# The transposes of the queries behind the whole projection, and the squares ahead of the copy of the queries, in a windowed-attention kernel on one core

## The reference, cut to what matters

```python
# layer 0: x = x + attention(group_norm(x)), in windows of 16 x 16 pixels, 8 heads of 12 channels
qkv = jnp.einsum('oc,bchw->bohw', w_qkv, x)
...
q = _l2norm(q).transpose(0, 1, 3, 2)
k = _l2norm(k)
ksum = k.sum(axis=-1) + EPS
tailor = 1.0 / (ws * ws + jnp.einsum('bhnc,bhc->bhn', q, ksum))
kv = jnp.einsum('bhmn,bhcn->bhmc', k, v)
attn = jnp.einsum('bhnm,bhmc->bhcn', q, kv)
attn = attn + v.sum(axis=-1, keepdims=True)
attn = attn * tailor[:, :, None, :]
...
y = jnp.einsum('oc,bchw->bohw', w_proj, out)
y = (y - mean) * jax.lax.rsqrt(var + BN_EPS)      # over the whole batch
# layer 1: x = x + wavelet_convolution(group_norm(x)), three Haar levels and a 5 x 5 depthwise convolution
```

## Time and profile before

| | |
|---|---|
| time, median of 3 runs | 11901.09 us (11895.07 to 11904.0) |
| time of the profiled execution | 11889.79 us, span 11888.0 us |
| granted TensorE clock, mean | 0.995 |
| TensorE busy | 10743.1 us, 90% |
| VectorE busy | 9364.9 us, 79% |
| ScalarE busy | 6980.0 us, 59% |
| GpSimd busy | 3393.1 us, 29% |

### The profile page before, as it was taken

One profiled execution on the slowest core, in us unless ns is written; L12 is line 12 of the kernel. 1 busy time (PEld: TensorE's weight loads), 2 busy tenths in 40 slices (PEclk: granted clock), 3 DMA queues, 4 the chain that ended last, 5 costly groups with the idle time before them and its releaser, 6 DMA issues. The chain is left out here.

```text
span 11888.0 us, 209663 instructions
## 1 busy us (share of the span) xinstructions
PE 10743.1 (90%) x68680; PEld 9231.7 (78%) x68680; DVE 9364.9 (79%) x16196; ACT 6980.0 (59%) x11653; POOL 3393.1 (29%) x2756
## 2 busy tenths in 40 slices
PE   0006999999999999999969999999999999999999
PEld 0005888888888888888858888888888888888888
DVE  6667888888888888888867777777777777777777
ACT  0005888888888888888844444555554444444554
POOL 1002444444444444444421222222222222222221
PEclk9999999999999999999979999999999999999999
DMA  9993222222222222222236666666666666666665
GB/s 233 217 219 88 80 80 78 82 75 85 75 85 75 85 75 79 81 76 84 75 76 147 147 147 149 149 148 148 149 149 149 147 147 147 147 147 147 149 149 125
DMA packets 1149490, 1452.08 MB, mean 122 GB/s; under 512 B 202079, under 2 KB 1111711, under 8 KB 1111967
## 3 DMA queue, kind: packets, MB, share of 16 engines
q1 hardware_dynamic: 1147743, 1442.74, 50.3%
q10 hardware_dynamic: 1376, 6.13, 0.1%
HBM read 1040.06 MB, written 408.56 MB: 122 GB/s over the span
## 5 line engine op out<-in xcount | busy, mean ns | idle before, releaser
L1076 PE MATMUL ps_w<-zb,mat 128*128 128x512 f32 x4800 | 1925.5, 401 | 0.1
L1078 PE MATMUL ps_w<-zb,mat 128*128 128x512 f32 x4800 | 1907.8, 397 | 0.0
L1077 PE MATMUL ps_w<-zb,mat 128*128 128x512 f32 x4800 | 1907.2, 397 | 0.0
L1029 ACT ACTIVATE z<-x,prm 64x384 f32<-64x384 f32 (+1 forms) x3072 | 1806.3, 659 | 54.7 <-DVE x L1139 47.0
L491 POOL CAST xn_hi<-xs 96x512 fp32r<-96x512 f32 x1024 | 882.6, 862 | 2854.7 <-PE ps_qkv L515 2067.2
L975 POOL CAST mat<-raw 128x1280 fp32r<-128x1280 f32 (+1 forms) x288 | 344.1, 1213 | 4452.5 <-DMA raw<-vec 2641.1
L1201 DVE SCALAR_TENSOR_TENSOR ob<-ps_w,prm,x 64x512 f32<-64x512 f32 x1920 | 1440.3, 750 | 182.6 <-PE ps_w L1119 143.6
L1139 DVE SCALAR_TENSOR_TENSOR x<-yb,prm,xb 128x1024 f32<-128x1024 f32 (+1 forms) x576 | 1120.7, 1997 | 387.0 <-DMA prm<-params 341.2
L513 PE MATMUL ps_qkv<-wqkv_hi,xn_hi 96*128 96x288 f32 x4096 | 1383.7, 338 | 23.3 <-POOL xn_lo L493 20.0
L493 POOL TENSOR_TENSOR xn_lo<-xs,xn_hi 96x512 fp32r<-96x512 f32 x1024 | 1297.8, 1267 | 82.2
L1049 ACT ACTIVATE ll<-ps_ll 128x512 f32<-128x512 f32 x192 | 115.1, 599 | 1882.7 <-PE ps_ll L1084 1882.7
(11 more groups left out here) (138 smaller groups left out, 24172.4 us busy)
## 6 DMA issues: line engine op xcount, KB each, us to landing
xs<-in_x SPq DMA_DIRECT2D x256, 1536.0 KB, 9.1
y_scratch<-ys SPq DMA_DIRECT2D x128, 1536.0 KB, 9.3
out<-ob SPq DMA_DIRECT2D x768, 208.0 KB
xb<-in_x SPq DMA_DIRECT2D x576, 256.0 KB
yb<-y_scratch SPq DMA_DIRECT2D x576, 256.0 KB
raw<-vec SPq DMA_DIRECT2D x192, 320.0 KB, 5.3
raw<-vec SPq DMA_DIRECT2D x384, 160.0 KB, 4.1
xb<-in_x SPq DMA_DIRECT2D x192, 240.0 KB
```

Source lines behind the costliest of these rows:

```text
L1029: last = nc.scalar.activation(z[q * WROWS:(q + 1) * WROWS, ts, b, :], x1[slot(k, g)][rows, pairs, b, q::2], ACT.Identity, scale=prm[k][row ...
L1076: mm(out_, w[HI], xx[HI], start=start, stop=False)
L1077: mm(out_, w[HI], xx[LO], start=False, stop=False)
L1078: return mm(out_, w[LO], xx[HI], start=False, stop=stop)
```

## The change

`project` no longer leaves its fourth group behind `turn_q`: TensorE issues all twelve matmuls of the projection, signals `qkv_ready`, and then issues the four transposes of the queries. On ScalarE `squares(u)` stands ahead of `copy_q(u-1)`. Nothing is added or removed, no wait and no buffer is changed.

```diff
@@ ScalarE, step @@
+                    if inside_(at, 0):
+                        squares(u, at == 0)
                     if inside_(at, 1):
                         copy_q(u - 1, (j - 1) % 2, at is not None and at - 1 < 2)
                     if inside_(at, 0):
-                        squares(u, at == 0)
                         copy_tok(u, j % 2, at is not None and at < 2)
@@ TensorE @@
-                def project(u, slot, gs):
+                def project(u, slot):
 
-                    for g in gs:
+                    for g in range(TG):
@@ TensorE, step @@
-                        project(u, j % 2, range(0, TG - 1))
+                        project(u, j % 2).then_inc(qkv_ready, 1)
                     if inside_(at, 1):
                         turn_q(u - 1, (j - 1) % 2, at is not None and at - 1 < 2)
-                    if inside_(at, 0):
-                        project(u, j % 2, range(TG - 1, TG)).then_inc(qkv_ready, 1)
```

## The result

The change makes the kernel slower: 11937.29 us (median of 7 runs, 11934.86 to 11944.88) against 11900.35 us (median of 7 runs, 11895.07 to 11904.0) for the kernel before. The ratio is 1.0033, 95% interval 1.0021 to 1.0045. The profiled execution took 11934.86 us against 11889.79, 45 us more. The difference is small, 0.3%, but clear of the runs' scatter: the slowest of the runs before is 31 us faster than the fastest after. In the rows of the experiments the numbers are again shifted by up to three, by each experiment's own edit; tiles and operations are the same.

The account below looks back on a forecast made before the run. TensorE's own work was taken to bound stage 2. Place 1 (22), place 3 (22), place 0 (22), turns (23) and ScalarE (-5) gave +84 us on 11889.8, 11974; predicted median 11985, 8-in-10 range 11910 to 12070.

Parts of the forecast that it names:

- the rival in which VectorE keeps places 0 and 3: Places 0 and 3: VectorE keeps its turn at both or one of them, 11941 or 11963 us; chance 0.22.
- GpSimd is first by 0.05 at place 1 and by a hair at places 0 and 3: Port race there: GpSimd's earlier cast starts before VectorE's line 621 or 642, so all three places are lost.
- the 0.45 us by which `qkv_ready` comes earlier: End of the projection, every place: last matmul starts at 2861.65 instead of 2862.10, without the transposes ahead of it.
- TensorE's order: Stage 2 steps: query transposes with `numerators` right behind take 0.44 us for four; new order costs nothing within 0.02 us.
- ScalarE: Squares ahead of `copy_q`: what follows starts 0.05 us earlier, GpSimd's late split of place 7 too, about 5 us gained.
- The price at place 1: Line 621 waits for GpSimd's cast, so line 551 starts 0.17 us later; 128 x 0.17 = 22 us.
- The turns: Loop's turns: line 621 waits for GpSimd's subtraction, line 558 comes later; a mean turn loses 0.77 us, 30 lose 23.
- Rival D: Not slower: at turns the fourth group's matmuls fill TensorE's wait, 30 x 0.39 = 12 us, giving 11884; chance 0.08.
- rival E: Places 2, 4 and 5: GpSimd wins the port there too, adding 78 us, 12063; chance 0.12.
- The price at place 0: Line 642 waits for GpSimd's cast, so line 558's transpose comes later; 0.22 us a step, 98 x 0.22 = 22 us.
- The lock's rule: Port pair shared by VectorE and GpSimd: whichever starts first holds it for the whole instruction, so places 0, 1, 3 are lost.

Follow-up runs that it names:

- e3: The full change with GpSimd's split also waiting for the transposes of the queries, against the kernel before: 11886.15 us against 11894.77, ratio 0.9994.
- e10: The full change with three tiny VectorE sums between line 621 and line 642, against the kernel before: 12036.1 us against 11896.13, ratio 1.0118.
- e5: The full change with three tiny VectorE sums behind the reciprocal of line 617, against the kernel before: 11940.67 us against 11899.15, ratio 1.0035.
- e7: The full change with GpSimd's split waiting for the query transposes and, at a strip's first unit, the unit keys; against the kernel before: 11868.56 us against 11899.15.
- e6: The kernel before with the split of a strip's first unit also waiting for the unit keys: 11878.76 us against 11899.15, ratio 0.9982.

## Why the prediction was wrong

The direction and the cause were right: the loss is GpSimd's earlier cast and subtraction, which take the port from VectorE. The size was not, and of the places one (place 0) was wrong and one (place 3) mostly so. I gave 11985 us (+84) with 11941 to 11963 for the rival in which VectorE keeps places 0 and 3; measured is 11937 (+37), or 45 us more between the profiled executions, for which the sum was made. That is close to the rival, which had 0.22.

The step that failed is "GpSimd is first by 0.05 at place 1 and by a hair at places 0 and 3". It rests on the 0.45 us by which `qkv_ready` comes earlier, read from one step. Over all steps the last projection matmul starts 1.98 us into the step before and 1.55 after, 0.43 us earlier. The cast starts 2.44 us into it before and 2.01 after (medians), 0.43 earlier; at place 0 it is 2.437 and 2.032, 0.41. Those two to four hundredths turn a race by a hair around. Counted in the trace after, VectorE lost at place 0 in 0 of 96 steps (I had all: 22 us; it is 2), at place 3 in 35 of 128 (22 us; it is 8), and at place 1 in 53 of 96 without those behind a turn, in 30 of 31 behind one (22 us together; it is 18). What splits place 1 is TensorE: the last projection matmul starts 1.53 or 1.54 us into the step in all 53 steps with VectorE held, and 1.56 or 1.57 us into it in 39 of the 43 others, as the two steps shown do (3042.37 and 2963.14). Some 44 us of the sum, places 0 and 3, hung on ties of 0.01 us, read from one step each, and were counted in full; 8 of them came, at place 3.

Point by point otherwise. TensorE's order: four transposes with `numerators` behind take 0.44 us, as taken. ScalarE: `copy_tok` starts 0.02 to 0.04 us earlier instead of 0.05, and place 7 gained 0.033 x 128 = 4 us instead of 5. The price at place 1: 0.17 forecast, 0.18 in the steps shown. With 53 of 96 steps and not all, place 1 comes to 18 us near the 22 forecast partly since the steps with VectorE let in lose 0.03 us too. The turns: 0.77 forecast, 0.75 measured, 23 us both, but in part by luck: the forecast path, line 620 behind the subtraction, is that of 23 turns in 29, and the other six lose nearly the same by line 641. Rival D made it hang on line 620 not being held at the turns; where it was not, the turn was lost all the same. Its gain of 0.39 us a turn is not to be had either, as e3 shows. Places 2, 4 and 5 stayed with VectorE, so rival E falls there; but what it describes, GpSimd getting in between the product of keys and line 641, is what happened at those six turns. The price at place 0 could not be seen in the change; in e10 it was 0.19 for 0.22.

The lock's rule in the Trainium skill (SBUF — State Buffer, "SBUF: two separate sides"), that whoever starts first gets the port pair, held in the trace after. There are 89 steps in which the cast's start lies 0.01 to 0.04 us ahead of line 620's, and 29 behind a turn with 0.23 us or more: all went to GpSimd. In the 260 steps in which it lies between level and 0.09 us behind, all went to VectorE. But a recorded start is not the moment of decision to a hundredth in every kernel: in e5, with three sums just ahead of the product, VectorE kept the port in 74 of 78 steps with the cast less than 0.03 us ahead, and GpSimd got it in all 146 with 0.03 us or more. In the change it was not the rule that failed, but the starts I put into it.

Still open: TensorE's projection takes some 0.025 us longer in a part of the steps after the change, most at place 0 and 1 (the last matmul of line 516 at 1.56 or 1.57 instead of 1.54 us into the step), in e3 too, and less in e7. Against the kernel before, places 0, 2, 4, 5 and 6 lose some 5 us in all, and no run tells its cause. Nor is it settled how the port goes when line 642 starts within 0.03 us of the cast right behind line 621: in e5 it kept the port in 43 steps with the cast's start level or up to 0.03 us ahead. In e10, with 0.07 to 0.20 us ahead, it was held in every step.

## What to carry to other kernels

A signal that comes earlier is an edit on every engine that waits for it. Before moving a producer, list who else its semaphore releases, and lay the released instruction's new start beside what the other engines do at that moment; here TensorE's wait fell by 12 us, and its steps grew by 50 us in sum, since an engine that is idle for 69% of the time was released 0.43 us earlier and got in the way of another one. And a filled wait is worth no more than the slack of what comes next on the path: 0.39 us of matmuls could give a turn 0.24 us at most and gave 0.15.

If two engines share a port, an extra wait that keeps the idle one away from the late one's critical instructions is an edit of a line or two, as e3, e6 and e7 show. And where a sum holds ties of a hundredth of a us, count them over all steps of the trace before they are priced in full: a single step showed all of places 0 and 3 lost, and it was none and a quarter.

## What the runs showed of the hardware

The port's outcome is sharp: in the trace after, 0.01 us of start decides whether line 620 takes 0.56 or 0.98 us, and 0.03 to 0.04 us on GpSimd (a write of 0.10 us) took VectorE's lost places at place 1 from 53 to 5 of 96. An instruction that waits for the port does not lose its place to one that asks later: at six turns GpSimd's subtraction waited 0.39 to 0.55 us for line 620 and then ran ahead of line 641. The loser's record ends a fixed time behind the winner's: in the trace after, the product of keys ends 0.41 to 0.42 us behind GpSimd's instruction, line 641 1.08 us behind it, and GpSimd's cast 0.47 us behind the product. Tiny instructions behind one whose result is awaited move little (three sums, 0.02 to 0.03 us); the same three between two instructions that run back to back move the second by 0.19 us.
